# Relative positions of two query rows in one product, in the second of two attention layers

## The reference

```
q, k, v = projections of the normalised x, per head        # layer 1 adds a LoRA term to q and v
attn  = (q * scale) @ k.T                                   # [head, 256, 256]
rel_h[h, w, kh] = sum_c q[h, w, c] * table_h[h - kh + 15, c]
rel_w[h, w, kw] = sum_c q[h, w, c] * table_w[w - kw + 15, c]
attn += rel_h[..., kh, None] + rel_w[..., None, kw]
out  = softmax(attn) @ v;  out = out @ wo + bo;  x = x + out
```

## Time and profile before

| | |
|---|---|
| median of 3 runs | 81.52 us (81.52 to 81.66) |
| the profiled execution, its own time | 81.54 us |
| its span, first to last instruction | 79.5 us |
| PE busy / weight loads (PEld) busy | 88% / 70% of the span |
| ACT / DVE / POOL busy | 65% / 58% / 15% |
| mean granted clock of TensorE | 0.998 of full |
| L736, 128 products of both layers | 8.0 us of busy PE, 7.9 us of weight loads |

### The profile page before, as it was taken

How to read it: one execution, slowest core, us unless ns; L and a number is a source line. 1 busy time by engine, 2 the same in 40 slices (tenths; PEclk the granted TensorE clock), 3 DMA queues, 4 the chain that set the end, 5 groups by cost and what they waited for, 6 DMA issues and landing times.

```text
span 79.5 us, 1633 instructions
## 1 busy us (share of the span) xinstructions
PE 69.9 (88%) x632; PEld 56.0 (70%) x632; DVE 45.7 (58%) x107; ACT 51.9 (65%) x98; POOL 11.8 (15%) x46
## 2 busy tenths in 40 slices
PE   4976989999978999979999999999878999988750
PEld 4955869998656975824768889999656994834630
DVE  4863999767846685422254649759576666323210
ACT  5429797999979787561330067799979787581420
POOL 5876400000121111000001100000031122000000
PEclk9999999999999999999999999999999999999999
DMA  0968000000000000000000000000000000000003
GB/s 13 278 167 264 12 0 8 0 0 0 0 4 0 8 4 0 0 0 0 0 8 0 0 0 0 0 0 0 8 0 0 0 0 0 0 8 0 0 0 99
DMA packets 1543, 1.75 MB, mean 22 GB/s; under 512 B 312, under 2 KB 1146, under 8 KB 1536
## 3 DMA queue, kind: packets, MB, share of 16 engines
q1 hardware_dynamic: 1536, 1.66, 7.2%
HBM read 1.46 MB, written 0.20 MB: 21 GB/s over the span
## 4 chain that ended last, share of the span: by engine, by line
PE 74%; DVE 10%; ACT 6%; issue 5%; POOL 1%; DVEq 0%; ACTq 0%
PE ps L736 10%; PE ps L633 8%; PE ps L579 7%; PE ps L593 7%; PE ps L615 6%; PE ps L716 6%; PE ps L503 5%; PE ps L564 4%; ACT qs L268 3%; PE ps L643 3%; PE ps L605 2%; PE ps L692 2%; PE ps L536 2%; PE ps L671 2%; PE ps L681 2%
## 5 line engine op out<-in xcount | busy, mean ns | idle before, releaser
L395 DVE TENSOR_REDUCE nm<-ps 128x2 f32<-128x512 f32 x24 | 15.5, 686 | 7.3 <-PE ps L579 7.1
L316 ACT ACTIVATE pt<-ps 128x1024 f32<-128x1024 f32 x12 | 12.3, 1024 | 1.4
L268 ACT ACTIVATE qs<-ps 64x512 fp32r<-64x512 f32 x20 | 11.8, 589 | 0.4
L503 PE MATMUL ps<-busy 128*128 128x128 bf16 x112 | 9.4, 243 | 1.5 <-DVE busy L365 1.1
L503 PEld LDWEIGHTS ps<-busy 128*128 128x128 bf16 x112 | 7.9, 112 | 2.5 <-DVE busy L365 1.0
L579 PE MATMUL ps<-ks,qs 128*128 128x256 f32 x48 | 8.9, 300 | 0.7 <-DVE nm L395 0.3
L736 PEld LDWEIGHTS ps<-zq,table 128*64 128x64 f32 x128 | 7.9, 138 | 0.7 <-issue 0.5
L736 PE MATMUL ps<-zq,table 128*64 128x48 f32 x128 | 8.0, 216 | 0.2 <-DVE zq L471 0.2
L254 POOL CAST nmhl<-nm 128x4 fp32r<-128x4 f32 x12 | 2.2, 187 | 40.1 <-DVE nm L395 40.1
L615 PE MATMUL ps<-nmt,ones 128*128 128x512 f32 x24 | 8.1, 418 | 0.1
L593 PE MATMUL ps<-qs,ks 128*128 128x256 f32 x48 | 8.1, 291 | 0.0
(11 more groups left out here) (94 smaller groups left out, 104.5 us busy)
## 6 DMA issues: line engine op xcount, KB each, us to landing
win<-in_w_in_dram SPq DMA_DIRECT2D x4, 216.0 KB
xt<-in_x_dram SPq DMA_DIRECT2D x1, 192.0 KB, 2.7
wout<-in_w_out_dram SPq DMA_DIRECT2D x2, 96.0 KB
out_dram<-res SPq DMA_DIRECT2D x1, 192.0 KB, 2.0
wout<-in_w_out_dram SPq DMA_DIRECT2D x2, 48.0 KB
rel_raw<-in_rel_dram SPq DMA_DIRECT2D x1, 62.0 KB, 2.9
win<-in_w_in_dram SPq DMA_DIRECT2D x2, 2.2 KB
wout<-in_w_out_dram SPq DMA_DIRECT2D x2, 0.8 KB
```

Of the source, the lines that this page charges most:

```text
L268: return act.activation(dst, src, ACT.Copy, scale=scale)
L316: act.activation(pt[:, p, :, :, :].rearrange("p a k t -> p a (k t)"), ps[:, ST_BANK[p % 2]:ST_BANK[p % 2] + 2, :], ACT.Exp, scale=SCALE[l] ...
L395: dve.tensor_reduce(nm[:, p, a, :], ps[:, S_BANK[a], :].rearrange("p (t k) -> p t k", k=T), AX.X, ALU.max, negate=True).then_inc(max_sb, 1)
L503: mm(ps[:, bank, 0:P], busy[:, :], busy[:, :], start=True, stop=True)
```

## The change

A new tile `windows` holds, for each high or low part and each `which`, eight stationary operands of 128 columns: two slices of table[1], eight rows apart, side by side. POOL writes it with four copies of 128 x 1024 each, after the table is there and before its first split_maxima(0, 0), and raises win_sb. Layer 0 is unchanged.

In layer 1 one product takes rows n and n + 8: 96 moving columns (both rows' queries) against the 128 stationary columns, and writes 128 partitions. Of each result only two quarters are used: partitions 64 to 127 of the first 48 columns (row n) and partitions 0 to 63 of the last 48 (row n + 8). There are 16 products for each `which`, and rel_ps is raised by 2 at the end of all sixteen, so both halves are waited for to the same point. ACT's moves 1 and 2 of layer 1 now come behind the copies rr_hi of which == 1 (KEYS_BEFORE_COLUMNS = [3, 1]).

```diff
--- before.py
+++ after.py
@@ -70,6 +70,8 @@
         rel_lo = sb("rel_lo", [P, LAYERS, 2 * R], F32R)
 
         table = [sb(f"table{l}", [P, 2, 2, R, G4], F32R) for l in range(LAYERS)]
+        windows = sb("windows", [P, 2, 2, HW // 2, 2, HW * G4], F32R)
 
         xt = [sb(f"xt{l}", [CH, NC, T]) for l in range(LAYERS)]
         stats = sb("stats", [CH, LAYERS, NC, 6])
@@ -126,6 +128,7 @@
             "wl_sb", "res_dve"))
         rstd_sb = sem("rstd_sb")
         nmt_zero = sem("nmt_zero")
+        win_sb = sem("win_sb")
 
 
 
@@ -148,6 +151,7 @@
                      ("r", 2, 0), ("r", 2, 1), ("q", 2, 0), ("q", 2, 1)]
         DVE_MOVES = [("k", 0, 1), ("q", 0, 1), ("r", 0, 1)]
 
+        KEYS_BEFORE_COLUMNS = [3, 1]
         BUSY_WITH_MAXIMA = [8, 5]
         BUSY_AT_START = 33
         BUSY_BEFORE_MEANS, BUSY_BEFORE_VARIANCE, BUSY_BEFORE_QK = [0, 5], [8, 9], [17, 14]
@@ -175,8 +179,14 @@
             sp.dma_start(out_tokens, res[:, :, :]).then_inc(stored, 16)
             sp.wait_ge(stored, 16)
 
-        def rel_src(which, half):
-
+        def rel_src(l, which, half):
+            if l == 1:
+                v = ps[64 - 64 * half:128 - 64 * half, REL_BANK + 2 * which:REL_BANK + 2 * which + 2, :].rearrange(
+                    "p b (i s) -> p (b i) s", s=P)[:, :, NG * HW * half:NG * HW * (half + 1)]
+                if which == 0:
+                    return v.rearrange("p h (g w) -> p g h w", g=NG)
+                return v.rearrange("p w (g h) -> p g h w", g=NG)
             v = ps[0:64, REL_BANK + 2 * which + half, 0:8 * NG * HW]
             if which == 0:
                 return v.rearrange("p (h g w) -> p g h w", g=NG, w=HW)
@@ -256,6 +266,15 @@
                 pool.tensor_tensor(nmhl[:, p, :, :, 1], by_tile, nmhl[:, p, :, :, 0].bitcast(F32),
                                    ALU.subtract).then_inc(nm_lo, 1)
 
+            pool.wait_ge(tab_sb, 4)
+            for part in range(2):
+                for which in range(2):
+                    first = table[1][:, part, which, 0:HW, :].rearrange("p r j -> p (r j)")
+                    rows, columns = first.ap
+                    overlapping = bass.AP(first.tensor, first.offset,
+                                          [rows, [G4, HW // 2], [HW // 2 * G4, 2], columns])
+                    pool.tensor_copy(windows[:, part, which, :, :, :], overlapping.bitcast(F32)).then_inc(win_sb, 1)
             for p in range(PAIRS):
                 split_maxima(0, p)
             inverse_deviation(1)
@@ -332,12 +351,12 @@
                         key_onehots(3)
                 for which in range(2):
                     for half in range(2):
-                        act.wait_ge(rel_ps, 4 * l + 2 * which + half + 1)
-                        copy(rel_dst(rr_hi, which, half), rel_src(which, half)).then_inc(rr_hi_sb, 1)
+                        act.wait_ge(rel_ps, 4 * l + 2 * which + (half + 1 if l == 0 else 2))
+                        copy(rel_dst(rr_hi, which, half), rel_src(l, which, half)).then_inc(rr_hi_sb, 1)
                     if which == 0:
-                        for n in range(3):
+                        for n in range(KEYS_BEFORE_COLUMNS[l]):
                             move(l, n)
-                for n in range(3, 13):
+                for n in range(KEYS_BEFORE_COLUMNS[l], 13):
                     move(l, n)
                 max_rows(l, 0)
                 for n in range(13, 15):
@@ -475,7 +494,7 @@
                     for half in range(2):
                         n = 4 * l + 2 * which + half + 1
                         dve.wait_ge(rr_hi_sb, n)
-                        dve.tensor_tensor(rel_dst(rr_lo, which, half), rel_src(which, half),
+                        dve.tensor_tensor(rel_dst(rr_lo, which, half), rel_src(l, which, half),
                                           rel_dst(rr_hi, which, half).bitcast(F32),
                                           ALU.subtract).then_inc(rr_lo_sb, 1)
                     if which == 0:
@@ -528,6 +547,33 @@
             def both(kind, g):
                 return (kind, g, 0), (kind, g, 1)
 
+            def relative_positions(l, which):
+                zv = zq[:, :, :].rearrange("p g (h w) -> p g h w", w=HW)
+                if l == 0:
+                    for i in range(HW):
+                        moving = zv[:, :, i, :] if which == 0 else zv[:, :, :, i]
+                        b, c = REL_BANK + 2 * which + i // 8, (i % 8) * NG * HW
+                        for part in range(2):
+                            last = mm(ps[0:64, b, c:c + NG * HW],
+                                      table[l][:, part, which, HW - 1 - i:2 * HW - 1 - i, :].rearrange(
+                                          "p r j -> p (r j)"), moving, start=(part == 0), stop=(part == 1))
+                        if i % 8 == 7:
+                            last.then_inc(rel_ps, 1)
+                    return
+                pe.wait_ge(win_sb, 4)
+                for n in range(HW // 2):
+                    if which == 0:
+                        moving = zv[:, :, n:HW:HW // 2, :].rearrange("p g s w -> p s g w")
+                    else:
+                        moving = zv[:, :, :, n:HW:HW // 2].rearrange("p g h s -> p s g h")
+                    b, c = REL_BANK + 2 * which + n // 4, (n % 4) * P
+                    for part in range(2):
+                        last = mm(ps[:, b, c:c + 2 * NG * HW],
+                                  windows[:, part, which, HW // 2 - 1 - n, :, :].rearrange("p s m -> p (s m)"),
+                                  moving, start=(part == 0), stop=(part == 1))
+                last.then_inc(rel_ps, 2)
             def key_rows(l, g):
                 if g == 0:
                     pe.wait_ge(made_pick, 2)
@@ -726,18 +772,7 @@
                     pe.wait_ge(tab_sb, 4)
                 pe.wait_ge(z_lo, 6 * l + NG)
                 for which in range(2):
-                    for i in range(HW):
-                        if which == 0:
-                            moving = zq[:, :, i * HW:(i + 1) * HW]
-                        else:
-                            moving = zq[:, :, :].rearrange("p g (h w) -> p g h w", w=HW)[:, :, :, i]
-                        b, c = REL_BANK + 2 * which + i // 8, (i % 8) * NG * HW
-                        for part in range(2):
-                            last = mm(ps[0:64, b, c:c + NG * HW],
-                                      table[l][:, part, which, HW - 1 - i:2 * HW - 1 - i, :].rearrange(
-                                          "p r j -> p (r j)"), moving, start=(part == 0), stop=(part == 1))
-                        if i % 8 == 7:
-                            last.then_inc(rel_ps, 1)
+                    relative_positions(l, which)
                     if which == 0:
                         key_rows(l, 0)
                         key_rows(l, 1)
```

## The result

The changed kernel took 83.39 us in the median of 4 runs (82.87 to 83.76) against 81.52 us (81.52 to 81.66): a ratio of 1.022 with the interval 1.016 to 1.028. It is slower, as forecast, but by more than the 1.35 us predicted, and 83.39 lies just above the upper end of the range, 83.3.

What follows compares the result with a forecast made beforehand. ACT's queue was taken to bound layer 1 up to turn_max: PE's 0.23 us hidden, POOL 0, ACT + 1.36 on the profiled 81.54 gave 82.9, less 0.02 for the median: 82.87 us; range 82.2 to 83.3.

Steps and rivals of the forecast that it cites:

- layer 0 unchanged: A sign of being right: layer 0 stays as before, with the sum set against the profiled execution of 81.54 us.
- The pair rr_hi: ACT's two copies of layer 1's group results were taken at 0.86 us, the second pair ending at 53.26.
- The copies from 128-partition results take a tenth longer: Possible extra price of copies after layer 1's new products: another 0.1 us.
- the break of PE ahead of turn_max: Sign in layer 1: PE's break before turn_max grows to near 0.9 us instead of 0.54.
- the pace of the products on zeros: Lower end kept for a new product's pace: 0.055 us, from bf16 products with 128 stationary columns.
- The pace of the loads: Layer 1's loads of 128 columns follow each other every 0.112 us, against 0.058 before.
- ACT's idle time: In layer 1 ACT idles about 0.8 us ahead of the second pair rr_hi.
- the two pitches behind it: Twelve moves instead of ten up to move 12 in layer 1: two pitches, 1.23 us later.
- The second rival: PE's own work is the bound before turn_max in layer 1: 81.3 us, down to 80; chance 0.04.
- POOL's copies: Four new copies early in the run, about 6 us together, done before POOL's next work at 21.48: cost nothing.
- the first scores wait for move 6: Layer 1's first scores follow move 6's end at 56.95, starting about 57.0 instead of 56.00.
- the third rival: The clock falls in layer 1's stretch before turn_max, TensorE getting 1.2 GHz for 2 to 4 us: 85 to 87; chance 0.05.

Runs made afterwards that it cites:

- e2_keys2: The changed kernel with two of ACT's moves instead of one ahead of layer 1's second pair rr_hi: 82.33 us, ratio 1.008.
- e3_keys3: The changed kernel with three of ACT's moves instead of one ahead of layer 1's second pair rr_hi: 82.45 us, ratio 1.007.
- e4_old_keys1: The kernel before, old products, with only one of ACT's moves ahead of layer 1's second pair rr_hi: 83.05 us, ratio 1.017.
- e8_same_side: The kernel before with ACT's moves 3 to 10 reordered so more copies follow one with the same partitions: 81.01 us, ratio 0.991.
- e6_again: The changed kernel run once more, nothing altered: 83.11 us, ratio 1.016 against the kernel before.
- e11_q_ahead: e9_both with ACT's move (q, 2, 0) ahead of the first nmt: 79.4 us, ratio 0.972 in two executions; median of all six 81.80.
- e5_high_part: The changed kernel without the table's low part in layer 1's products, 8 products instead of 16 per which: 82.03 us, ratio 1.005.
- e7_dve_move: The kernel before with one of ACT's moves, (r, 2, 1), given to DVE in both layers: 80.3 us, ratio 0.982.
- e9_both: The kernel before with (r, 2, 1) given to DVE and ACT's moves in the partition-keeping order: 79.8 us, ratio 0.977.
- e10_changed_relieved: The changed kernel with three moves ahead, (r, 2, 1) on DVE and the partition-keeping order: 82.73 us, ratio 1.014, clock held in no execution.

## Why the prediction was wrong

**The step that failed** is the one that set the sum against a single profiled execution, with "layer 0 unchanged" taken as "the first 10 us unchanged". Layer 0 has the same instructions, but TensorE's clock rises at about 4 us in one execution and past 9 us in another, which costs 0.6 to 0.8 us. The four executions of the kernel before that were at hand agreed within 0.14 us, and I took that for its spread; over 28 it was 16 early to 12 late. By their spans, two of the four of the changed kernel were late, which puts its median between the levels. The range had no term for it.

That this made the difference between inside and outside the range is in part luck: 83.39 is 0.09 above its upper end, and the next six executions of the same kernel have their median at 83.11, inside it.

**A term was mis-sized.** The pair rr_hi takes 0.99 us where I used the 0.86 of the old pair. The two halves now lie in different partitions (64 to 127 and 0 to 63), and the second copy no longer starts before the first has ended. That is 0.13 on the path: move 12 ends at 61.57 - 0.78 = 60.79, against 60.65 forecast. "The copies from 128-partition results take a tenth longer" had this size, but only for the range.

**A sign that failed** is the break of PE ahead of turn_max: 0.9 us was forecast, and it stayed at 0.54 (the row at 61.13). The prediction took PE's ready time, 58.85, for its own. But scores_t(1, 1), the products right ahead of the break, wait for ACT's move 10, two moves before move 12. The rows of ACT's move 10 (in the second fence merged with move 11) and of the loads of scores_t(1, 1), before and then changed:

```profile
57.47 0.59 ACT L268 ACTIVATE qs<-ps 64x512 fp32r<-64x512 f32 x1
58.11 0.54 PEld L593 LDWEIGHTS ps<-qs,ks 128*128 128x128 f32 x4
```

```profile
59.74 1.21 ACT L287 ACTIVATE qs<-ps 64x512 fp32r<-64x512 f32 x2
60.39 0.53 PEld L639 LDWEIGHTS ps<-qs,ks 128*128 128x128 f32 x4
```

They start 0.05 or 0.06 after move 10 has ended (58.06, and 59.74 + 0.59 = 60.33). So the break comes from where the two waits stand in ACT's queue, and it does not tell how much sooner PE could be ready.

**A reading that was off, to no effect:** the pace of the products on zeros, 0.055, used the mean of 0.243 of both clock levels. With 0.219 it is (0.84 - 0.219) / 11 = 0.056.

**Right, and shown:**
- The pace of the loads, 0.112 forecast and 0.111 measured. The groups took 1.99 and, with the first load at 51.13, 2.02 us up to their end; forecast 1.99 and 2.00. The trace does not agree with the 81 ns for a pair of load and matmul in the Trainium skill, "TensorE: Matmul & The Clock Gate", section Back-to-back issue gap: for this type of operand it shows 111 ns, with 96 moving columns.
- ACT's idle time, 0.8 forecast and 0.81 measured, and the two pitches behind it. `e2_keys2` and `e3_keys3` move the time of the changed kernel, and `e4_old_keys1` that of the kernel before, by the order of ACT's queue alone.
- That ACT's queue sets the pace up to turn_max: halved products gain nothing in the order that the change chose (0.3 us by the estimate above in the other), and one move less gains a pitch in each layer. The second rival falls.
- POOL's copies are hidden to within 0.1 us; they take 1.0 us each.
- That the first scores wait for move 6. They came at 58.15 - 0.78 = 57.4, against 57.0: move 6 ended at 57.88 - 0.78 = 57.10, 0.14 later than forecast by the slower pair, and the scores started 0.27 after it, where 0.05 was taken. What fills the 0.27 is not shown.
- The clock did not fall in the changed kernel's stretch before turn_max (granted 1.00 there, and a mean of 0.991 or more in all its ten executions), so the third rival did not come about.

With the clock's rise early, the change costs 1.5 us; by the experiments 0.9 of it is the place of the two moves, net of the later pair, and the remaining 0.6 is the wait of both halves for the end and the copies that no longer overlap.

## What to carry to other kernels

Before halving the number of matmuls by doubling the stationary operand, look at what one load costs: where loads set the pace, as here, 16 loads of 128 columns take what 32 of 64 took, and the result comes in one piece at the end instead of in two. Look also at the engine that empties PSUM: if its queue has no gap, the time follows its order and its count of copies, and a move given to an engine with a gap is worth more than a shorter product. Run the kernel before often enough to see both of its levels before taking one execution as the base. And look at how often the clock holds in a faster version, not only at its best time.

## What the runs showed of the hardware

**Copies overlap only when they stay in their partitions.** In the changed kernel, both copies of the second pair rr_hi of layer 0 read from partition 0 and write from 64; in layer 1 the first reads from 64 and the second from 0. ACT's pair of layer 0, then DVE's pairs rr_lo of both layers:

```profile
16.83 0.86 ACT L287 ACTIVATE rr_hi<-ps 64x384 fp32r<-64x384 f32 x2
```

```profile
17.35 1.02 DVE L497 TENSOR_TENSOR rr_lo<-ps,rr_hi 64x384 fp32r<-64x384 f32 x2 [0.82 <-ACT rr_hi L287]
...
53.70 1.14 DVE L497 TENSOR_TENSOR rr_lo<-ps,rr_hi 64x384 fp32r<-64x384 f32 x2 [0.41 <-ACT rr_hi L287]
```

ACT needs 0.99 (its row at 53.18, above) instead of 0.86, and DVE 1.14 instead of 1.02. DVE's second copy also needs ACT's second, but that has ended at 53.69 + 0.48 = 54.17; the copy starts at 53.70 + 1.14 - 0.56 = 54.28, just after DVE's first has ended at 54.26. The Trainium skill, "VectorE: DVE Perf Modes", section Two Vector instructions with no wait between them, says that an instruction whose input or output starts in another quadrant of partitions than the one ahead waits until all earlier ones have finished. DVE's rows agree, and ACT's show the same there, in `e8_same_side` too, where the order alone gained 0.5 us.

**The clock's rise at the start** differs by 5 us between executions (about 4 us in the profile of the kernel before, past 9 in that of the changed one, between 5.3 and 5.6 in that of `e6_again`), and the granted clock does not show it; the pace of equal products does (0.056 against 0.104 us).

**The clock's fall between the layers.** In the profile of `e11_q_ahead`, PE is busy without a gap around it and still gets half the clock:

```profile
42.00:44.00 2.00, 2.00 (x14) 1.47 (x14) 1.50 (x5) 0.00 (x0) 0.70 (x1) 0.60 0.00 0
44.00:46.00 2.00, 2.00 (x12) 1.80 (x10) 0.37 (x1) 0.00 (x0) 0.00 (x0) 0.50 0.00 0
```

PE works just before and around the fall, 40 to 45 us, on LoRA products over 4 partitions, products of 2 columns and products on zeros. Counting executions with a mean granted clock below 0.98, it happened in 7 of 63 of the kernel before, in none of 10 of the changed one, in 1 of 12 with the copies alone, in 2 of 10 each of `e2_keys2`, `e3_keys3` and `e5_high_part`, in 2 of 7 of `e8_same_side`, but in 3 of 6, 2 of 4, 4 of 4 and 4 of 6 of `e7_dve_move`, `e9_both`, `e10_changed_relieved` and `e11_q_ahead`. So the kernels that take a move off ACT lose it more often; why is open. Whether other work in that place would hold the clock was not tried; it is what stands between `e11_q_ahead` and a dependable 79.4 us.
